# Turned context kept by ScalarE's copies and read back three stages later, and a logarithm with an exponential in place of root and reciprocal

## What is computed

```python
def layer_norm(x, g, b):
    mu = jnp.mean(x, axis=-1, keepdims=True)
    var = jnp.var(x, axis=-1, keepdims=True)
    return (x - mu) * jax.lax.rsqrt(var + EPS) * g + b
...
# L3_xattn; x is the context, latents is the normalised x of the program
xn = layer_norm(x, gamma_x, beta_x)
ln = layer_norm(latents, gamma_l, beta_l)
q = (ln @ Wq).reshape(b, m, h, d)
kv_x = xn @ Wkv
k_x = rope_rotate_k(k_x)
...
attn = jax.nn.softmax(sim, axis=-1)
out = jnp.einsum('bhij,bhjd->bhid', attn, v)
return out @ Wo
```

## Time and profile before

| | us |
|---|---|
| median of 3 runs | 2768.2 (2767.07 to 2770.44) |
| the profiled execution | 2769.61 |
| its span on the core | 2767.4, mean granted TensorE clock 0.979 |
| TensorE busy | 2582.4 (93% of the span), 16423 matmuls |
| VectorE busy | 1769.8 (64%) |
| ScalarE busy | 1589.7 (57%) |
| GpSimd busy | 1376.6 (50%) |
| L0_xattn, whole stage | from about 5 to about 500; a steady unit 27.1 |
| L3_xattn, whole stage | from 1869 to about 2625 |

### The profile page before, as it was taken

The page is one execution under the profiler, slowest core; times in us unless marked ns, Lnnn a source line. Parts: engine busy times, 40 slices in busy tenths (PEclk is TensorE's granted clock), DMA queues, the critical chain, the costliest instruction groups (busy, mean ns, idle before and its releaser), DMA issues. The chain is left out here.

```text
span 2767.4 us, 43589 instructions
## 1 busy us (share of the span) xinstructions
PE 2582.4 (93%) x16423; PEld 2159.1 (78%) x16423; DVE 1769.8 (64%) x3649; ACT 1589.7 (57%) x2786; POOL 1376.6 (50%) x1094
## 2 busy tenths in 40 slices
PE   5999999898999999999988878998999999999878
PEld 4899998686999999999987756885677777777647
DVE  7878885455555555555545435428888888888572
ACT  3888887234766666666643232425666666666432
POOL 0878776111767666777722000206665666666140
PEclk9999999999999999999999999999999999999999
DMA  4233331022011111111006081203000000000000
GB/s 114 81 102 96 87 98 38 15 58 64 25 37 37 37 36 37 37 37 37 13 6 184 4 257 34 62 1 81 25 14 25 26 13 25 14 25 2 3 1 8
DMA packets 209436, 130.94 MB, mean 47 GB/s; under 512 B 22720, under 2 KB 201424, under 8 KB 209232
## 3 DMA queue, kind: packets, MB, share of 16 engines
q1 hardware_dynamic: 209232, 128.22, 16.3%
HBM read 113.51 MB, written 13.64 MB: 46 GB/s over the span
## 5 line engine op out<-in xcount | busy, mean ns | idle before, releaser
L847 POOL TENSOR_TENSOR L_xattn_held<-L_xattn_held,L_xattn_shift 128x512 f32<-128x512 f32 (+1 forms) x613 | 783.3, 1318 | 242.7 <-ACT L_xattn_shift L769 242.7
L575 PEld LDWEIGHTS L_xattn_acc<-L_xattn_rows,L_xattn_held 128*128 128x128 f32 (+2 forms) x5120 | 618.3, 192 | 37.0 <-DVE L_xattn_mixed L954 13.6
L575 PE MATMUL L_xattn_acc<-L_xattn_rows,L_xattn_held 128*128 128x129 f32 (+2 forms) x5120 | 629.5, 276 | 5.2 <-DVE L_xattn_mixed L954 5.2
L975 DVE TENSOR_TENSOR L_xattn_running<-L_xattn_ring,L_xattn_running 128x512 f32<-128x512 f32 (+1 forms) x384 | 263.8, 687 | 257.4 <-PE L_xattn_ring L557 247.1
L759 ACT ACTIVATE L_xattn_held<-L_xattn_held 128x512 f32<-128x512 f32 (+2 forms) x640 | 400.6, 631 | 0.2
L1618 POOL TENSOR_TENSOR L_xattn_projected<-L_xattn_along,L_xattn_crossed 128x512 f32<-128x512 f32 (+1 forms) x256 | 271.5, 1072 | 256.1 <-DVE L_xattn_crossed L1685 254.1
L752 ACT COPY L_xattn_held<-L_xattn_ring 128x512 f32<-128x512 f32 (+1 forms) x416 | 243.3, 585 | 210.6 <-DVE L_xattn_running L975 189.9
L555 PE MATMUL L_xattn_ring<-L_xattn_queries_hi,L_xattn_keys_hi 128*128 128x512 f32 (+2 forms) x640 | 282.2, 441 | 4.0 <-DVE L_xattn_keys_lo L875 2.0
L557 PE MATMUL L_xattn_ring<-L_xattn_queries_hi,L_xattn_keys_lo 128*128 128x512 f32 (+2 forms) x640 | 254.3, 397 | 0.0
L556 PE MATMUL L_xattn_ring<-L_xattn_queries_lo,L_xattn_keys_hi 128*128 128x512 f32 (+2 forms) x640 | 253.6, 396 | 0.0
L1322 PE MATMUL L_xattn_sums<-L_xattn_probT,L_xattn_rows 128*128 128x256 f32 (+2 forms) x896 | 242.7, 382 | 0.6 <-ACT L_xattn_mixed L1507 0.6
(11 more groups left out here) (525 smaller groups left out, 4856.0 us busy)
## 6 DMA issues: line engine op xcount, KB each, us to landing
first_loads_fresh<-in_ctx_turned SPq DMA_DIRECT2D x16, 800.5 KB, 4.3
opening_keysT<-in_ctx_turned SPq DMA_DIRECT2D x8, 1601.0 KB, 7.6
L_xattn_raw<-in_ctx SPq DMA_DIRECT2D x16, 768.0 KB
context_normalised<-L_xattn_fresh SPq DMA_DIRECT2D x16, 768.0 KB
L_xattn_rows<-context_normalised SPq DMA_DIRECT2D x16, 768.0 KB
L_xattn_rows<-in_ctx SPq DMA_DIRECT2D x16, 768.0 KB
opening_rows<-in_ctx SPq DMA_DIRECT2D x16, 768.0 KB
L_xattn_xhat<-context_normalised SPq DMA_DIRECT2D x16, 768.0 KB
```

The lines of the kernel that those rows point to most:

```text
L575: mm = nc.tensor.matmul(acc[:, c // 2, c % 2 * WIDE:(c % 2 + 1) * WIDE], held[0:n, u % 2, k, c * P:(c + 1) * P], rows[0:n, b % 2, k, :], s ...
L847: nc.gpsimd.tensor_tensor(tile, tile, shift[0:keys_of_tile[k]], ALU.subtract).then_inc(shifted, 1)
L975: seen = nc.vector.tensor_tensor(most, bank, most, ALU.max)
```

## The change

Five edits. First, in L0_xattn ScalarE copies every turned chunk from `spare` to a new SBUF tile `xhatT` before it rounds it (60 copies: 45 of 512 columns, 15 of 65). Second, SyncE stores `xhatT` of each batch from 1 on to a new DRAM tensor `context_turned` (15 stores of 128 x 1601, 820 KB each), behind the store of the rows and ahead of the load of the rows. ScalarE waits for the store before it overwrites `xhatT`. Third, in `context_root` the root becomes a logarithm, a drain and an exponential of minus one half of it, all on ScalarE, and VectorE's reciprocal goes. Fourth, in L3_xattn SyncE loads `context_turned` to `staged`, ScalarE applies gain and shift there and rounds to `keys_hi`. TensorE's turns of the context (13 for each of 15 batches) go, ScalarE's copies to `rows` go, and GpSimd scales and shifts the rows in place, at t = 3 and then at t = 0 of the next batch. The gain and the shift are also loaded as columns, ahead of the weights, and what waited for the gains now waits for these too. Fifth, the matmuls of `keep_clock_pe` go from 24 to 16 in L2_xattn and from 40 to 22 in L2_attn.

```diff
 def context_root(b):
     act.wait_ge(cvar_ready, b + 1)
-    nc.scalar.activation(cstd[:], mean_var[:, :, 1], ACT.Sqrt, bias=core.eps(EPS_5), scale=1.0)\
-        .then_inc(cstd_ready, 1)
+    nc.scalar.activation(cstd[:], mean_var[:, :, 1], ACT.Ln, bias=core.eps(EPS_5), scale=1.0)
+    act.drain()
+    nc.scalar.activation(crstd[:], cstd[:], ACT.Exp, scale=-0.5).then_inc(cstd_ready, 1)
...
 def invert_std(b):
     dve.wait_ge(cstd_ready, b + 1)
-    nc.vector.reciprocal(crstd[:], cstd[:])
-    dve.drain()
...
                 if normed:
-                    round_chunk(b, c, take()).then_inc(hi_ready, 1)
+                    bank = take()
+                    if c == 0 and b >= 2:
+                        act.wait_ge(turned_stored, 16 * (b - 1))
+                    c0, n = CTX_CHUNKS[c]
+                    nc.scalar.copy(xhatT[:, c0:c0 + n], bank[:, 0:n]).then_inc(turned_kept, 1)
+                    round_chunk(b, c, bank).then_inc(hi_ready, 1)
                     return
...
                     if b + 1 < BATCHES:
                         next_xhat(b + 1)
+                        sp.wait_ge(turned_kept, len(CTX_CHUNKS) * (b + 1))
+                        sp.dma_start(core.ctx_turned[b + 1], xhatT[:]).then_inc(turned_stored, 16)
...
             def keep_context(pair, parity, c):
                 c0, n = CTX_CHUNKS[c]
-                done = NC * (pair * 2 + parity - 1) + c
-                if done >= 2:
-                    act.wait_ge(keys_split, done - 1)
-                bank = take()
-                emptied(nc.scalar.copy(turned[:, c % 2, 0:n], bank[:, 0:n]))
+                part = staged[:, c0:c0 + n]
+                if c == 0:
+                    act.wait_ge(staged_loaded, 16 * (pair * 2 + parity))
+                nc.scalar.activation(part, part, ACT.Identity, bias=shift_col[:], scale=gain_col[:])
                 act.drain()
-                nc.scalar.copy(keys_hi[:, parity, c0:c0 + n], turned[:, c % 2, 0:n]).then_inc(keys_rounded, 1)
+                nc.scalar.copy(keys_hi[:, parity, c0:c0 + n], part).then_inc(keys_rounded, 1)
...
-                    if t == R - 2 and not no_context:
-                        scale_context(b + 2, parity)
-                    if t == R - 1 and not no_context:
-                        shift_context(parity)
+                    if t == 0 and b:
+                        shift_rows(b)
+                    if t == R - 1 and not last:
+                        scale_rows(b + 1)
...
-            keep_clock_pe(nc, core, sums[:, 0:2 * P], 24)
+            keep_clock_pe(nc, core, sums[:, 0:2 * P], 16)
...
-            keep_clock_pe(nc, core, bank[1][:, 0:2 * P], 40)
+            keep_clock_pe(nc, core, bank[1][:, 0:2 * P], 22)
```

101 lines of the change are left out of this document (46 added, 55 removed).

## The result

| | median of the runs, us | ratio to before, 95% interval |
|---|---|---|
| before | 2770.4 (2767.1 to 2771.6, 5 runs) | 1 |
| changed | 2758.6 (2754.0 to 2759.1, 5 runs) | 0.9958 [0.9944, 0.9971] |
| changed, timed again (e8) | 2759.6 (2751.6 to 2763.0, 7 runs) | 0.9959 [0.9943, 0.9974] |

By the ratios 11 to 12 us came off (by the medians of the second series 9.3), where 22 were forecast. The sign and the range were right, the size was not. The profiled execution took 2758.6, its span 2756.8. I laid both traces side by side at the first and last clock-keeping matmuls, which mark the ends of the stages. Columns: start before, then how much later the changed kernel is there, and what the stretch above added.

A forecast was written before the change was run, and what follows sets the result against it. TensorE was taken to bound L0_xattn (busy throughout) and L3_xattn (97.5 of 100 us), VectorE's loop next. L3_xattn −26, clock-keeping matmuls −11 and L0_xattn +14 made −23 from 2769.6: forecast 2746 us, range 2732 to 2762.

The forecast's parts named there:

- L3_xattn: Stage losing the context's turns: 3.66 us less per pair of batches, 7.5 pairs, −26 with the opening, range −20 to −31.
- The loop: In L3_xattn, VectorE and GpSimd rotating keys set their own pace, about 10.46 us a slot.
- the slot behind the queries: In L3_xattn, the slot following the one with queries was put at 9.75 to 9.79 us.
- L3_xattn shrinking by under 20: Stated sign that the prediction is wrong: L3_xattn gets less than 20 us shorter.
- Rival (1): L3_xattn slots stay near 10.7 as ScalarE or GpSimd replace the turn: 2.6 less per pair, 2752 us; chance 0.2.
- The table loads: L0_xattn: a second load delays the queries' cast; with the first chunk's 0.2, 1.2 us in six odd units, 7.2.
- The copies: L0_xattn: ScalarE's copy ahead of the rounding exposes 0.15 us in each of 8 even units, 1.2 in all.
- The chain round the bank: L0_xattn: fill, ScalarE's queue, new copy, rounding to next fill estimated at 3.8 us, against TensorE's step of 3.9.
- The opening of L0_xattn: Units 0 to 2, where TensorE already waits: queries' delay, exposed copies and one load add 6 us.
- The clock-keeping matmuls: Fewer in L2_xattn (−3.5) and L2_attn (−7.3): together −11 us, between −9 and −11.5, no clock cost taken.
- The store: L0_xattn: 820 KB ahead of the rows' load lands them 3 to 4.3 us later, hidden by some 5 of slack.
- Rival (3): L0_xattn's store delays the rows past GpSimd's slack, 3.5 us in each of 15 units: 2797 to 2798; chance 0.05.

The follow-up runs named there:

- e8: The changed kernel unaltered, timed once more against the kernel before: 2759.6 us, ratio 0.9959.
- e13: Changed kernel, in L3_xattn without the second of VectorE's two crossed products of the keys' third piece, from the second slot on: 2724.1 us (one run).
- e15: Changed kernel with VectorE's reciprocal of the sums in L3_xattn moved behind the third piece of the rotation: 2744.9 us, ratio 0.9911.
- e1: Kernel before with only the fewer clock-keeping matmuls (16 and 22 in place of 24 and 40): 2760.2 us, ratio 0.9967.
- e2: Kernel before with only the logarithm and exponential in L0_xattn: 2774.3 us, ratio 1.0026.
- e3: Kernel before with only ScalarE's copies of the turned chunks and SyncE's stores of them, root and reciprocal kept: 2782.0 us, ratio 1.0052.
- e4: Changed kernel with root and reciprocal put back in L0_xattn: 2752.5 us, ratio 0.9944.
- e7: e4 with ScalarE's copy freeing the spare bank, and rounding and split reading the kept tile behind a drain: 2779.5 us, ratio 1.0041.

## Why the prediction was right or wrong

- **L3_xattn (−26 forecast, −13.1 in the trace; the step that failed).** The term of the sum was mis-sized: eight slots were to be 84.8 and are 86.2, which is 2.25 and not 3.66 less. The loop was named, and its slots are as forecast (10.41 to 10.55 for 10.37 to 10.46). The error is in the slot behind the queries, put at 9.75 to 9.79 because the last batch has 9.79 behind a long slot. That row is the first slot of a batch, behind an output. Where queries are made that same slot is 10.91, and the next is 10.70. The output's slot is 12.24, at the upper bound and not at 11.95. These two make 0.95 + 0.29 (against 9.75 and 11.95), and the other slots add 0.17. At 7.5 pairs that is 10.6 us of the missing 13. The prediction named L3_xattn shrinking by under 20 as a sign that it is wrong, and that sign came.

The ring does not hold the slot behind the queries. With the ring shortened it stays at 10.67 (e13) and 10.69 (e15). In it TensorE waits 0.76 for the probabilities that ScalarE normalises, and ScalarE comes to them only behind its copies of the new queries. In the changed kernel (ScalarE, then TensorE):

```profile
2213.58 2.50 ACT L1478 COPY L_xattn_queries<-L_xattn_asked 32x512 f32<-32x512 f32 x4
...
2216.58 1.69 ACT L1491 ACTIVATE L_xattn_prob<-L_xattn_prob,L_xattn_rinv 128x1665 f32<-128x1665 f32 x1
...
2218.32 0.66 PE L1313 MATMUL L_xattn_bank_a<-all_ident,L_xattn_prob 128*128 128x128 f32 x4 [0.76 <-ACT L_xattn_prob L1491]
```

The kernel before has this wait too, 0.74 in the same slot. No run moved it, so that it sets the slot is read from the trace and not shown.

The rest of the 13 is in the opening and the first batch, and most of it is of the execution. Together they took 69.4 before (69.4 to 70.7 with e1, e2 and e3) and 73.5 in this trace, but 72.3 in e4, 70.7 in e8 and 69.7 in e7, with the same code of the stage. The whole stage took 752.4 to 753.6 in the four traces with its old code (before, e1, e2, e3) and 736.4 to 739.3 in the four with the new one: on average 15.1 less, where this one pair of traces has 13.1.
- **Rival (1)** gave 2.6 less for a pair and 2752. It is the nearest to what came (2.25 and 2758.6), but for another reason. In six of eight slots neither ScalarE nor GpSimd took the turn's place, but a ring through TensorE, VectorE and GpSimd that was there before. Only in the slot behind the queries does TensorE wait for ScalarE. I should have given it more than 0.2: the one slot below 10.3 in the loop of before (9.73) stands behind two with turns (12.24 and 10.72), and those were to go.
- **The table loads (7.2 forecast in six odd units).** Right: 1.25 each against 1.2, with two loads as the order of the program had them, and the Trainium skill's rule not borne out.
- **The copies (0.15 in even units).** The number was right, 0.13, by luck: it holds only with the logarithm beside it. Alone the copies cost 0.65 in each unit (e3). The chain round the bank was put at 3.8, under TensorE's step of 3.9. Its own terms (0.60 for the fill, 0.69 and 0.62 in the trace for the score copy and the exponential, 0.55 and 1.71) add up to 4.2, over the step, and that sum had the cost in it. I priced each part against the trace of before and added. That the earlier second load gives ScalarE back 0.5 us at the first chunk was no step of mine.
- **The opening of L0_xattn (+6).** One pair of traces can't settle it. Against the trace of before the changed kernel reached unit 3 at +1.5 in one execution and at +6.8 in another, and e1, with untouched L0_xattn, at −5.2. On average the seven traces with the changed L0_xattn are at +3.1 there (1.1 to 6.8) and the six with the untouched one at −2.5 (−5.2 to +1.5). The difference, 5.6, bears the forecast out.
- **The clock-keeping matmuls (−11).** Right: e1 gives 9.1 by its ratio, and the two stages are 5.4 and 5.8 shorter in the changed kernel's trace. Over all traces, eleven with fewer and seven with all of them, it is 4.3 and 7.7 (3.5 and 7.3 forecast). The clock was not lost behind them: L2_ffn, the next stage, took 114.2 on average with fewer and 114.4 with all.
- **The store.** Right: the rows came 2.6 later (3 to 4.3 forecast), and the 5 us of slack were not overrun. Rival (3) fell.
- **The sum.** Wrongly sized, and L3_xattn is the whole of it. On average over the traces the end of L0_xattn came 15.4 later (510.4 to 516.8 in seven with the changed stage, 494.4 to 501.2 in six with the untouched one; 14 forecast), the two stages with clock-keeping matmuls were 12.0 shorter (11), and L3_xattn 15.1 shorter (26): 11 missing there, and 11 in all. In the one pair of traces above L1_xattn was 2.6 longer besides, and 2.1 of that is in its opening, where the granted clock was 1.00 before and 0.79 after (here 8 us of each):

```profile
676.00:684.00 8.00, 5.43 (x33) 4.59 (x34) 6.50 (x11) 5.45 (x12) 0.11 (x1) 1.00 0.31 102
```

```profile
686.90:694.90 8.00, 5.67 (x24) 4.55 (x23) 5.05 (x10) 4.47 (x9) 0.00 (x0) 0.79 0.32 102
```

In each of the two stretches TensorE waits 2.33 us for VectorE's maxima. L1_xattn was 2.0 to 5.1 longer in eight of eleven traces with the copies, and 2.1 or 2.2 longer in three of six without them. Its code is the same in all, so L0_xattn's new code is not shown to be the cause.

## What to carry to other kernels

When work is taken from the busiest engine, find the ring that comes next, from one wait to the same wait a turn later, with the time of every station. The piece that stands ahead of the wait belongs to the ring, and what VectorE does behind it doesn't, however busy VectorE is. Here a reciprocal of 0.2 us in the ring was worth 9.5 us in L3_xattn, and 195 transposes outside it 15. A slot that also does rare work, as here the one behind the queries, is to be priced from a row of that same slot. Parts of a change that share an engine's queue are to be priced together, in the order in which they will stand there.
